# A graph network on one core: another order for ScalarE and VectorE in the last pass over the edges

## The chip, the core and the metric

The kernel runs on one core of a Trainium2 chip. Five engines work side by side and meet by semaphores: TensorE (PE, matrix products and transposes), VectorE (DVE), ScalarE (ACT), GpSimd (POOL, here the issuer of gathers and scatters) and SyncE (SP, the issuer of plain transfers). Each engine runs its own instructions strictly in the order in which they were written. The metric is device time in microseconds for one execution, lower is better.

## The reference

50,000 nodes carry 256 features, 12,500 edges carry 128. Two layers follow one another, each with a residual and a layer norm. The first weighs each edge's source row by a softmax over the edges with the same `dst`. The second averages, for each node that is named in `src`, its neighbours' rows, and is the one that matters here:

```python
    agg = segment_sum(x[nbr], dst, num_segments=n)        # dst = src list, nbr = dst list
    mean = agg / jnp.maximum(cnt, 1.0)[:, None]
    return x @ W1.T + b1 + mean @ W2.T + b2
...
edge_index = jnp.stack([src, dst])
x = _layernorm(x + _L0_gnn_ref(x, edge_index, edge_attr_128, ...), axis=-1)
x = _layernorm(x + _L1_gnn_ref(x, ..., edge_index), axis=-1)
```

## The kernel before, in words

The kernel sorts the edges by either end, runs the first layer over the edges sorted by `dst`, then a dense stage over all nodes as if none had a neighbour (`dense`, 98 groups of 512 rows), and last the SRC pass (`by_src`), which computes the rows of the nodes that do have neighbours again and scatters them over the dense result. Only the SRC pass is touched here.

The SRC pass goes over the sorted edges in Q = 25 groups of 512 (four tiles of 128, GT = 4). A group q has two inputs: the *own rows* (z rows of the nodes in `src`, gathered by POOL into `xin`, `own_rows(q)`) and the *neighbour rows* (gathered into `X` beforehand). Both want a layer norm. Own rows: VectorE takes their moments (`moments`, L971, "own statistics"), ScalarE the root (`root`, L591), VectorE the reciprocal and the offset (`invert` L985 and the `nmr` product, "own offsets"), ScalarE the normalised rows in place (L770). Then TensorE turns them (`turn_pair`, L1378), ScalarE copies the turned rows from PSUM (`own_copy`, L586), and they are a term of the products (L1389). Neighbours: VectorE makes the selection matrices `csel` and `sel` (`select_src`, L1063 and L1065) and a weight per row, ScalarE weighs the rows (`weigh_neighbours`, L750), TensorE sums them by runs (L1533), VectorE adds what is carried from one tile to the next (`sums_with_carry`, L1079 and, through the helper of L801, L1082). The products give r; VectorE takes its moments ("ended products", L971 on a bank), ScalarE the root, VectorE the reciprocal (L1250), ScalarE scales r into `yout` (`y_rows`, L596), POOL scatters it (L487).

TensorE's step q runs in two halves, p = 0 and 1, of two tiles each: turn the own rows of q-1, sum the neighbours of q, multiply q-1. VectorE and ScalarE have a step q each, 27 in all, since r of group q-2 is finished in it. So in one step an engine touches groups q-2 to q+2, and the order in which it does so is written out by hand in the three functions `by_src`. A wait stands with the instruction that needs it; whatever was written behind it waits too.

POOL's order: gather the own rows of group s+3, then scatter group s-2, in step s. A gather waits until TensorE has turned the group whose buffer it takes (four buffers); a scatter waits for `y_rows`. SP brings the sorted keys (`kB`) two groups ahead.

Of the kernel before, what the change touches and what calls it, by code (L numbers as in the profile page):

```python
# [5 lines left out]
P = 128  # L6
D = 256
DE = 128
GT = 4
# [8 lines left out]
ALU = mybir.AluOpType  # L18
# [15 lines left out]
def wait(eng, sem, value):  # L34

    if isinstance(value, int) and value <= 0:
        return
    eng.wait_ge(sem, value)
# [19 lines left out]
def build(nc, x, src, dst, edge_attr, Wn, bn, We, be, attn, W1, b1, W2, b2, out):  # L58
# [4 lines left out]
    Q = T // GT  # L63
# [19 lines left out]
    with ExitStack() as ctx:  # L83
        def sb(name, shape, dt=F32):
            return ctx.enter_context(nc.sbuf_tensor(name, shape, dt))

        def sem(name):
            return ctx.enter_context(nc.semaphore(name))

        def sems(name, n):  # L90
            return [sem(f"{name}{i}") for i in range(n)]
# [99 lines left out]
        stats = sb("stats", [P, 6, GT, 3])  # L191
        std = sb("std", [P, 6, GT])
        rstd = sb("rstd", [P, 6, GT])
        nmr = sb("nmr", [P, 2, GT])
# [87 lines left out]
        s_ost = sem("own_stats")  # L282
        s_osq = sem("own_std")
# [4 lines left out]
        s_est = sem("edge_r_stats")  # L288
        s_esq = sem("edge_r_std")
        s_enm = sem("edge_r_scales")  # L290
        s_ey = sem("edge_y_ready")
        s_xs = sems("own_z_rows_gathered", 4)
# [7 lines left out]
        s_onm = sem("own_offsets")  # L300
# [24 lines left out]
        def counted(m, u, off, n):  # L325

            return m * (4 // n) + (u + off) // n

        def in_range(q, lo, hi):
            return not isinstance(q, int) or lo <= q < hi  # L330
# [4 lines left out]
        def own_rows(q, u=0):  # L335

            if isinstance(q, int):
                return (agg[0], agg[1], aggn)[q] if q < EARLY else xin[(q + G) % 4]
            return xin[(u + G) % 4]

        def rbank(h_par, p):
            return bank[4 + 2 * h_par + p]
# [236 lines left out]
        def _(act):  # L579
# [9 lines left out]
            def root(slot, ready, n, done, rows=P):  # L589
                act.wait_ge(ready, n)  # L590
                a.activation(std[0:rows, slot, :], stats[0:rows, slot, :, 2], ACT.Sqrt, bias=eps_c[0:rows],  # L591
                             scale=1.0 / D).then_inc(done, 1)

            def y_rows(h_par, hu, slot, done, bank_of, rows=P, js=range(GT)):
                for j in js:
                    a.activation(yout[hu][0:rows, j, :], bank_of(j // 2)[0:rows, (j % 2) * D:(j % 2 + 1) * D],  # L596
                                 ACT.Copy, scale=rstd[0:rows, slot, j:j + 1]).then_inc(done, 1)
# [127 lines left out]
            def root_neighbours(q, u):  # L725
                root(4 + u % 2, s_nst, q + 1, s_nsq)
# [18 lines left out]
            def weigh_neighbours(q, u):  # L745
                act.wait_ge(s_nw, q + 1)
                wait(act, s_agg[SRC], 2 * (q - 1))
                for j in range(GT):
                    rows = X[:, bass.ds(q * GT + j, 1), 0:D].rearrange("p a c -> p (a c)")
                    a.activation(X[:, u % 2 * GT + j, 0:D], rows, ACT.Copy,  # L750
                                 scale=rstd[:, 4 + u % 2, j:j + 1]).then_inc(s_stage, 1)

            weigh_neighbours(0, 0)

            def by_src(q, m, u):
                def own_copy(p):
                    if in_range(q, 1, Q + 1):
                        turned_copy(2 + p, bank[p], s_tc, 2 * (q - 1) + p + 1,
                                    [(s_er, 2 * (q - 2) + p + 1)], s_tcc, 1.0)
                if in_range(q, 0, Q):  # L760
                    root(u % 2, s_ost, q + 1, s_osq)
                own_copy(0)
                if in_range(q, 2, Q + 2):
                    root(2 + u % 2, s_est, q - 1, s_esq)
                own_copy(1)
                if in_range(q, 0, Q):
                    act.wait_ge(s_onm, q + 1)
                    for j in range(GT):
                        row = own_rows(q, u)[:, j, 0:D]
                        a.activation(row, row, ACT.Identity, bias=nmr[:, u % 2, j:j + 1],  # L770
                                     scale=rstd[:, u % 2, j:j + 1]).then_inc(s_ex1, 1)
                if in_range(q, 0, Q - 1):
                    weigh_neighbours(q + 1, u + 1)
                if in_range(q, 0, Q - 2):
                    root_neighbours(q + 2, u)
                if in_range(q, 2, Q + 2):
                    hu = (u - 2) % 4
                    act.wait_ge(s_enm, q - 1)
                    if isinstance(q, int) and q < 6:
                        act.wait_ge(s_yst[hu], 16 * len(range(hu, G, 4)))  # L780
                    wait(act, s_ysc[hu], 16 * GT * counted(m, u, -2, 4))
                    y_rows(0, hu, 2 + u % 2, s_ey, lambda p: rbank(u % 2, p))
            steps(act, Q + 2, 4, 8, 5, by_src)


        @block.vector
        def _(dve):
# [12 lines left out]
            def stt(o, i0, s, i1, o0, o1, **kw):  # L800
                return v.scalar_tensor_tensor(out=o, in0=i0, scalar=s, in1=i1, op0=o0, op1=o1, **kw)  # L801
# [172 lines left out]
            def halves(psum):  # L974
                return psum.rearrange("p (j c) -> p j c", j=2)

            def moments(slot, pair_of, rows, done):

                pair_stats(slot, rows, 0, pair_of(0))
                pair_stats(slot, rows, 1, pair_of(1)).then_inc(done, 1)  # L980

            n_m = [0] * 4

            def invert(slot, rows, h):
                v.reciprocal(rstd[0:rows, slot, :], std[0:rows, slot, :]).then_inc(s_rc[slot], 1)  # L985
                dve.wait_ge(s_rc[slot], h)
# [65 lines left out]
            def select_src(q, m, u, off):  # L1052

                par, turn = (u + off) % 2, counted(m, u, off, 2)
                slot = 4 + par
                now = bass.ds(q * GT, GT)
                dve.wait_ge(s_nsq, q + 1)
                v.reciprocal(rstd[:, slot, :], std[:, slot, :]).then_inc(s_rc[slot], 1)
                dve.wait_ge(s_rc[slot], turn + 1)
                v.tensor_tensor(rstd[:, slot, :], rstd[:, slot, :], weight[:, now], ALU.mult).then_inc(s_nw, 1)  # L1060
                dve.wait_ge(s_kb3[SRC][par], 16 * (turn + 1))
                wait(dve, s_agg[SRC], 2 * (q - 1))
                v.tensor_tensor(csel[par][:], kB[par][:], prevk[SRC][:, now].unsqueeze(2).to_broadcast([P, GT, P]),  # L1063
                                ALU.is_equal)
                v.tensor_tensor(sel[par][:], kB[par][:], keyc[SRC][:, now].unsqueeze(2).to_broadcast([P, GT, P]),  # L1065
                                ALU.is_equal).then_inc(s_sel[SRC], 1)
# [35 lines left out]
            def neighbour_stats(q, u):  # L1102
                for p in range(2):
                    ins = pair_stats(4 + u % 2, P, p, X[:, bass.ds(GT * q + 2 * p, 2), 0:D])
                ins.then_inc(s_nst, 1)
# [122 lines left out]
            steps(dve, G, 4, 4, 6, dense, (HOOK, HOOK + APART))  # L1228
            n_m = [G // 2 + (i % 2 < G % 2) for i in range(4)]

            def by_src(q, m, u):
                slot = u % 2
                if in_range(q, 0, Q):
                    own = own_rows(q, u)
                    dve.wait_ge(s_xs[u], 16 * GT * (m + 1))
                    moments(slot, lambda p: own[:, 2 * p:2 * p + 2, 0:D], P, s_ost)
                if in_range(q, 0, Q - 1):
                    select_src(q + 1, m, u, 1)
                if in_range(q, 0, Q):
                    dve.wait_ge(s_osq, q + 1)  # L1240
                    invert(slot, P, n_m[slot] + counted(m, u, 0, 2) + 1)
                    stt(nmr[:, slot, :], stats[:, slot, :, 1], -1.0, rstd[:, slot, :], ALU.mult, ALU.mult).then_inc(s_onm, 1)
                if in_range(q, 2, Q + 2):
                    dve.wait_ge(s_er, 2 * (q - 2) + 2)
                    moments(2 + slot, lambda p: halves(rbank(slot, p)[:, :]), P, s_est)
                if in_range(q, 0, Q - 2):
                    neighbour_stats(q + 2, u)
                if in_range(q, 2, Q + 2):
                    dve.wait_ge(s_esq, q - 1)
                    v.reciprocal(rstd[:, 2 + slot, :], std[:, 2 + slot, :]).then_inc(s_enm, 1)  # L1250
                if in_range(q, 0, Q):
                    sums_with_carry(q, u)
            steps(dve, Q + 2, 4, 4, 5, by_src)


# [309 lines left out]
```

## Time and profile before

| | |
|---|---|
| Time, median of 3 runs | 1405.91 us (1404.85 to 1406.67) |
| The profiled execution | 1415.9 us, span 1414.1 us |
| PE, DVE, ACT, POOL busy | 85%, 71%, 53%, 53% of the span |
| The SRC pass in the span | from about 1056 us to the end |

The span is one profiled execution, about 10 us longer than the median. The shares are means over stages with different limits; the SRC pass is read by itself. Busy times of TensorE count a pipelined instruction as busy until its modelled end, so starts are a better measure than ends. The chain that ended last names, in order of time, the piece of work that everything after it waited for.

### The profile page before, as it was taken

Reading aid. Unit: us, or ns where it says so; the run is one execution under the profiler, and the core shown is the slowest. Engines: PE = TensorE matmul, PEld = TensorE weight load, DVE = VectorE, ACT = ScalarE, POOL = GpSimd, SP = SyncE. Lnnn points to the kernel's source line nnn. Section 1 sums busy time; section 2 is a strip of 40 time slices with the busy share of each in tenths; the row PEclk is TensorE's granted clock in tenths of the full one; section 3 lists DMA queues with packets and bytes.
Section 4 is the critical chain, followed back from the end, with each engine's and each line's share of the span. In section 5 each row is a group of like instructions: output and inputs, shape, how many; then the busy total and the mean of one; then the engine's idle time right before and its main releaser. Section 6 shows DMA issues by size and latency. Waiting matters only on the chain.

```text
span 1414.1 us, 25043 instructions
## 1 busy us (share of the span) xinstructions
PE 1201.5 (85%) x6829; PEld 1046.3 (74%) x6829; DVE 1002.8 (71%) x3483; ACT 745.4 (53%) x1743; POOL 751.7 (53%) x731
## 2 busy tenths in 40 slices
PE   5988968991099999949999999999988888888884
PEld 5977857880078888838888888888877777777773
DVE  8377897989455555349999999999985556555551
ACT  3754664550034444427777766667674544545442
POOL 1047772777767777744444106555541555555533
PEclk9989999996589999979999999999998889988887
DMA  6868887979436666657777768999961323222211
GB/s 213 272 150 206 208 225 184 272 231 348 171 68 93 101 94 92 72 137 246 239 240 245 248 241 296 310 321 325 325 238 51 91 94 94 86 91 88 93 47 43
DMA packets 118160, 254.11 MB, mean 180 GB/s; under 512 B 23705, under 2 KB 63272, under 8 KB 118084
## 3 DMA queue, kind: packets, MB, share of 16 engines
q1 hardware_dynamic: 75738, 187.26, 41.8%
q0 software_dynamic: 40128, 64.45, 20.1%
q10 hardware_dynamic: 2218, 1.53, 0.3%
q8 instruction: 30, 0.49, 0.2%
q14 instruction: 46, 0.38, 0.1%
HBM read 175.67 MB, written 130.44 MB: 216 GB/s over the span
## 4 chain that ended last, share of the span: by engine, by line
PE 70%; DVE 11%; DMA 6%; ACT 5%; issue 5%; POOL 1%; SPq 0%; DVEq 0%; ACTq 0%; POOLq 0%
PE bank L1389 41%; PE bank L1378 8%; PE bank L1366 5%; DVE stats L971 4%; PE bank L1438 3%; PE bank L1288 3%; PE bank L1442 3%; DMA X<-in_x,idx_src 3%; DVE X L798 2%; ACT aggn L633 2%; PE bank L1533 2%; ACT sel L687 1%; PE bank L1325 1%; DVE xT L801 1%; DVE xin L798 1%
## 5 line engine op out<-in xcount | busy, mean ns | idle before, releaser
L1389 PE MATMUL bank<-w1T,xT 128*128 128x256 f32 x1968 | 480.3, 392 | 2.0 <-ACT yout L596 2.0
L1389 PEld LDWEIGHTS bank<-w1T,xT 128*128 128x128 f32 x1968 | 378.0, 197 | 56.6 <-ACT xT L586 3.0
L494 POOL DMA_INDIRECT order_scratch<-pay,rank_i x200 | 194.6, 973 | 220.6 <-DVE xin L798 90.3
L586 ACT ACTIVATE xT<-bank 128x512 f32<-128x512 f32 x296 | 176.7, 598 | 91.5 <-PE bank L1378 87.0
L596 ACT ACTIVATE yout<-bank,rstd 128x256 f32<-128x256 f32 x492 | 203.8, 480 | 0.7 <-DVE rstd L1037 0.5
L591 ACT ACTIVATE std<-stats,eps_c 128x4 f32<-128x4 f32 x271 | 80.5, 298 | 230.5 <-DVE stats L971 230.4
L534 POOL DMA_INDIRECT z_scratch<-xin,idx_out x100 | 156.3, 1563 | 53.8 <-ACT xin L713 30.6
L971 DVE BATCH_NORM_STATS2 stats<-bank 128x6 f32<-128x512 f32 x246 | 167.9, 691 | 10.2 <-PE bank L1389 10.1
L971 DVE BATCH_NORM_STATS2 stats<-xin 128x6 f32<-128x512 f32 x240 | 154.6, 686 | 22.6 <-DMA xin<-z_scratch 22.6
L1389 PE MATMUL bank<-w2T,xT 128*128 128x256 f32 x400 | 126.7, 446 | 50.4 <-ACT xT L586 41.8
L487 POOL DMA_INDIRECT out_rows<-yout,idx_out x100 | 102.4, 1024 | 107.7 <-ACT yout L596 83.0
L1366 PE MATMUL bank<-sel,agg 128*128 128x196 f32 x800 | 157.0, 341 | 0.1
L801 DVE SCALAR_TENSOR_TENSOR xT<-csel,xT,bank 128x128 f32<-128x128 f32 x198 | 55.6, 342 | 139.4 <-PE bank L1389 126.3
L1378 PE MATMUL bank<-ident,xin 128*128 128x128 f32 x960 | 128.9, 274 | 19.6 <-DVE xin L798 19.6
L1378 PEld LDWEIGHTS bank<-ident,xin 128*128 128x128 f32 x960 | 114.3, 142 | 34.4 <-issue 19.9
L1389 PEld LDWEIGHTS bank<-w2T,xT 128*128 128x128 f32 x400 | 84.9, 222 | 69.2 <-issue 31.8
L798 DVE TENSOR_SCALAR xin<-xin,stats,rstd 128x256 f32<-128x256 f32 x392 | 136.0, 409 | 0.1
L1366 PEld LDWEIGHTS bank<-sel,agg 128*128 128x128 f32 x800 | 134.4, 196 | 0.6 <-DVE bank L801 0.3
L484 POOL DMA_INDIRECT X<-z_scratch,idx_dst x100 | 96.1, 961 | 69.1 <-DVE xin L798 29.7
L484 POOL DMA_INDIRECT X<-in_x,idx_src x100 | 99.0, 990 | 51.2 <-issue 20.7
L484 POOL DMA_INDIRECT xin<-z_scratch,idx_src x88 | 84.7, 963 | 76.2 <-PE bank L1378 53.8
L1288 PE MATMUL bank<-X 128*128 128x196 bf16 x800 | 96.2, 255 | 28.8 <-ACT sel L687 18.6
(249 smaller groups left out, 1765.7 us busy)
## 6 DMA issues: line engine op xcount, KB each, us to landing
z_scratch<-in_x SPq DMA_DIRECT2D x125, 400.0 KB
xin<-z_scratch SPq DMA_DIRECT2D x97, 512.0 KB, 4.8
out_rows<-yout SPq DMA_DIRECT2D x97, 512.0 KB, 3.7
kB<-sorted_scratch SPq DMA_DIRECT2D x50, 256.0 KB, 3.4
yout<-low_digits_scratch SPq DMA_DIRECT2D x50, 128.0 KB
yout<-keys_scratch SPq DMA_DIRECT2D x50, 128.0 KB, 5.7
yout<-in_edge_attr SPq DMA_DIRECT2D x12, 512.0 KB, 6.2
order_scratch<-pay,rank_i POOLq DMA_INDIRECT x200
```

The lines of the kernel that those rows point to most:

```text
L484: g.indirect_dma_start(out=dst_ap, out_offset=None, in_=table, in_offset=where).then_inc(s, 16)
L487: g.indirect_dma_start(out=table, out_offset=where, in_=src_ap, in_offset=None, bounds_check=N - 1, oob_is_err=False).then_inc(s, 16)
L494: g.indirect_dma_start(out=order_dram[k], out_offset=bass.IndirectOffsetOnAxis(ap=rank_i[k][:, t:t + 1], axis=0), in_=pay[:, t, :], in_off ...
L534: g.indirect_dma_start(out=z_dram, out_offset=column(idx_out[DST], GT * q + j), in_=xin[q % 4][:, j, :], in_offset=None, compute_op=ALU.ad ...
L586: a.activation(xT[dst_i][:].rearrange("p a b c -> p (a b c)"), src_bank[:, :], ACT.Copy, bias=raised).then_inc(copied, 1)
L596: a.activation(yout[hu][0:rows, j, :], bank_of(j // 2)[0:rows, (j % 2) * D:(j % 2 + 1) * D], ACT.Copy, scale=rstd[0:rows, slot, j:j + 1]). ...
L798: return v.tensor_scalar(o, i, s1, s2, o0, o1) if o1 is not None else v.tensor_scalar(o, i, s1, s2, o0)
L971: return v.bn_stats(stats[0:rows, slot, 2 * p:2 * p + 2, :].rearrange("p j s -> p (j s)"), pair.rearrange("p j c -> p c j"))
L1288: ins = mm(o[:, b * HC:(b + 1) * HC], onehot_lo[:, t, b * P:(b + 1) * P], onehot_hi[:, t, :], start=False, stop=False, skip_group_check=True)
L1366: ins = mm(bank[3 + t % 4][:, 0:HC], onehotT[n % 2][:, b, j * P:(j + 1) * P], table[i % 2][:, b, :], start=b == 0, stop=b == 1)
L1378: ins = tr(o[:, at:at + n], buf[0:n, 2 * p + jj, c * P:(c + 1) * P], ident[0:n, 0:n])
L1389: ins = mm(to, buf[:, jj, c, 0:n], w[:, c, :], start=not bias and i == 0 and c == 0, stop=i == len(terms) - 1 and c == 1)
```

## The change

In the SRC pass three orders are written anew. VectorE takes the own statistics and offsets of group q+1 in step q, with those of group 0 ahead of the loop; its step begins with the moments of the ended products. ScalarE begins its step with the first copy of the turned rows, normalises the own rows, takes the two roots, splits `y_rows` in two around the second copy, and weighs the neighbours last. TensorE, POOL and SP keep their order, and no instruction is added or taken away except that `y_rows` is issued in two parts of two rows.

```diff
--- before.py
+++ after.py
@@ -750,6 +750,7 @@
                     a.activation(X[:, u % 2 * GT + j, 0:D], rows, ACT.Copy,
                                  scale=rstd[:, 4 + u % 2, j:j + 1]).then_inc(s_stage, 1)
 
+            root(0, s_ost, 1, s_osq)
             weigh_neighbours(0, 0)
 
             def by_src(q, m, u):
@@ -757,29 +758,34 @@
                     if in_range(q, 1, Q + 1):
                         turned_copy(2 + p, bank[p], s_tc, 2 * (q - 1) + p + 1,
                                     [(s_er, 2 * (q - 2) + p + 1)], s_tcc, 1.0)
-                if in_range(q, 0, Q):
-                    root(u % 2, s_ost, q + 1, s_osq)
+
+                def last_step(p):
+                    if in_range(q, 2, Q + 2):
+                        y_rows(0, (u - 2) % 4, 2 + u % 2, s_ey, lambda b: rbank(u % 2, b), P, (2 * p, 2 * p + 1))
                 own_copy(0)
-                if in_range(q, 2, Q + 2):
-                    root(2 + u % 2, s_est, q - 1, s_esq)
-                own_copy(1)
                 if in_range(q, 0, Q):
                     act.wait_ge(s_onm, q + 1)
                     for j in range(GT):
                         row = own_rows(q, u)[:, j, 0:D]
                         a.activation(row, row, ACT.Identity, bias=nmr[:, u % 2, j:j + 1],
                                      scale=rstd[:, u % 2, j:j + 1]).then_inc(s_ex1, 1)
+                if in_range(q, 2, Q + 2):
+                    root(2 + u % 2, s_est, q - 1, s_esq)
                 if in_range(q, 0, Q - 1):
-                    weigh_neighbours(q + 1, u + 1)
-                if in_range(q, 0, Q - 2):
-                    root_neighbours(q + 2, u)
+                    root((u + 1) % 2, s_ost, q + 2, s_osq)
                 if in_range(q, 2, Q + 2):
                     hu = (u - 2) % 4
                     act.wait_ge(s_enm, q - 1)
                     if isinstance(q, int) and q < 6:
                         act.wait_ge(s_yst[hu], 16 * len(range(hu, G, 4)))
                     wait(act, s_ysc[hu], 16 * GT * counted(m, u, -2, 4))
-                    y_rows(0, hu, 2 + u % 2, s_ey, lambda p: rbank(u % 2, p))
+                last_step(0)
+                own_copy(1)
+                last_step(1)
+                if in_range(q, 0, Q - 1):
+                    weigh_neighbours(q + 1, u + 1)
+                if in_range(q, 0, Q - 2):
+                    root_neighbours(q + 2, u)
             steps(act, Q + 2, 4, 8, 5, by_src)
 
 
@@ -1228,26 +1234,35 @@
             steps(dve, G, 4, 4, 6, dense, (HOOK, HOOK + APART))
             n_m = [G // 2 + (i % 2 < G % 2) for i in range(4)]
 
+            def own_stats(q, m, u):
+                own = own_rows(q, u)
+                dve.wait_ge(s_xs[u % 4], 16 * GT * (m + u // 4 + 1))
+                moments(u % 2, lambda p: own[:, 2 * p:2 * p + 2, 0:D], P, s_ost)
+
+            def own_offsets(q, m, u):
+                slot = u % 2
+                dve.wait_ge(s_osq, q + 1)
+                invert(slot, P, n_m[slot] + counted(m, u, 0, 2) + 1)
+                stt(nmr[:, slot, :], stats[:, slot, :, 1], -1.0, rstd[:, slot, :], ALU.mult, ALU.mult).then_inc(s_onm, 1)
+
+            own_stats(0, 0, 0)
+            own_offsets(0, 0, 0)
+
             def by_src(q, m, u):
                 slot = u % 2
-                if in_range(q, 0, Q):
-                    own = own_rows(q, u)
-                    dve.wait_ge(s_xs[u], 16 * GT * (m + 1))
-                    moments(slot, lambda p: own[:, 2 * p:2 * p + 2, 0:D], P, s_ost)
-                if in_range(q, 0, Q - 1):
-                    select_src(q + 1, m, u, 1)
-                if in_range(q, 0, Q):
-                    dve.wait_ge(s_osq, q + 1)
-                    invert(slot, P, n_m[slot] + counted(m, u, 0, 2) + 1)
-                    stt(nmr[:, slot, :], stats[:, slot, :, 1], -1.0, rstd[:, slot, :], ALU.mult, ALU.mult).then_inc(s_onm, 1)
                 if in_range(q, 2, Q + 2):
                     dve.wait_ge(s_er, 2 * (q - 2) + 2)
                     moments(2 + slot, lambda p: halves(rbank(slot, p)[:, :]), P, s_est)
-                if in_range(q, 0, Q - 2):
-                    neighbour_stats(q + 2, u)
+                if in_range(q, 0, Q - 1):
+                    own_stats(q + 1, m, u + 1)
                 if in_range(q, 2, Q + 2):
                     dve.wait_ge(s_esq, q - 1)
                     v.reciprocal(rstd[:, 2 + slot, :], std[:, 2 + slot, :]).then_inc(s_enm, 1)
+                if in_range(q, 0, Q - 1):
+                    select_src(q + 1, m, u, 1)
+                    own_offsets(q + 1, m, u + 1)
+                if in_range(q, 0, Q - 2):
+                    neighbour_stats(q + 2, u)
                 if in_range(q, 0, Q):
                     sums_with_carry(q, u)
             steps(dve, Q + 2, 4, 4, 5, by_src)
```

On VectorE one step near the end of the loop held this before (`xin3` own rows of group q, `bank6` and `bank7` the products of group q-2, `X` neighbours of group q+2, `xT` turned sums of group q):

```order
L971 BN_STATS stats<-xin3 128x6 x2
L1058 RECIPROCAL rstd<-std 128x4
L1060 TENSOR_TENSOR rstd<-rstd,weight 128x4
L1063 TENSOR_TENSOR csel0<-kB0,prevk1 128x512
L1065 TENSOR_TENSOR sel0<-kB0,keyc1 128x512
L985 RECIPROCAL rstd<-std 128x4
L801 SCALAR_TENSOR_TENSOR nmr<-stats,rstd 128x4
L971 BN_STATS stats<-bank6 128x6
L971 BN_STATS stats<-bank7 128x6
L971 BN_STATS stats<-X 128x6 x2
L1250 RECIPROCAL rstd<-std 128x4
```

The same step in the changed kernel (`xin0` are now the own rows of group q+1):

```order
L977 BN_STATS stats<-bank6 128x6
L977 BN_STATS stats<-bank7 128x6
L977 BN_STATS stats<-xin0 128x6 x2
L1260 RECIPROCAL rstd<-std 128x4
L1064 RECIPROCAL rstd<-std 128x4
L1066 TENSOR_TENSOR rstd<-rstd,weight 128x4
L1069 TENSOR_TENSOR csel0<-kB0,prevk1 128x512
L1071 TENSOR_TENSOR sel0<-kB0,keyc1 128x512
L991 RECIPROCAL rstd<-std 128x4
L807 SCALAR_TENSOR_TENSOR nmr<-stats,rstd 128x4
L977 BN_STATS stats<-X 128x6 x2
```

The moments of the two banks stand first and the own statistics behind them, where before the own statistics stood first; `L1250` moved from behind the neighbours' moments to ahead of the selection.

On ScalarE a step of the loop before (`xT2` and `xT3` take the two halves of the turned rows, the three roots on `std` are those of the own rows, of the ended products and of the neighbours):

```order
L591 ACTIVATE std<-stats,eps_c 128x4
L586 ACTIVATE xT2<-bank0 128x512
L591 ACTIVATE std<-stats,eps_c 128x4
L586 ACTIVATE xT3<-bank1 128x512
L770 ACTIVATE xin2<-xin2,nmr,rstd 128x256 x4
L750 ACTIVATE X<-X,rstd 128x256 x4
L591 ACTIVATE std<-stats,eps_c 128x4
L596 ACTIVATE yout2<-bank4,rstd 128x256 x2
L596 ACTIVATE yout2<-bank5,rstd 128x256 x2
```

and in the changed kernel:

```order
L586 ACTIVATE xT2<-bank0 128x512
L770 ACTIVATE xin2<-xin2,nmr,rstd 128x256 x4
L591 ACTIVATE std<-stats,eps_c 128x4 x2
L596 ACTIVATE yout2<-bank4,rstd 128x256 x2
L586 ACTIVATE xT3<-bank1 128x512
L596 ACTIVATE yout2<-bank5,rstd 128x256 x2
L750 ACTIVATE X<-X,rstd 128x256 x4
L591 ACTIVATE std<-stats,eps_c 128x4
```

The root of the own rows stood ahead of the first copy and that of the ended products ahead of the second; now no root stands ahead of the first copy, both stand between the normalising and `y_rows`, and the weighing of `X` stands behind all copies.

## Rows read from the trace of the kernel before

**Rows 1.** The chain that ended last: start us, length us, what; SRC pass.

```profile
1063.29 3.69 PE bank L1389 x16
...
1171.09 3.72 PE bank L1389 x16
...
1181.04 1.22 DVE stats L971 x2
1182.49 0.58 ACT xT L586
1183.11 5.41 PE bank L1389 x16
1188.52 0.44 PE bank L1378 x4
1188.96 0.89 PE bank L1533 x8
1189.85 3.53 PE bank L1389 x16
...
1386.34 3.69 PE bank L1389 x16
```

**Rows 2.** Busy time by window: TensorE's granted clock after DVE, ACT and POOL.

```profile
700.00:1050.00 350.00, 347.93 (x1924) 307.49 (x1924) 325.39 (x820) 246.46 (x640) 150.84 (x158) 1.00 0.82 279
...
1185.00:1186.00 1.00, 1.00 (x4) 0.82 (x3) 1.00 (x3) 0.30 (x1) 0.69 (x2) 0.50 0.83 205
```

**Rows 3.** Timeline of one step, ScalarE and VectorE: start us, length us, instruction.

```profile
1189.00 0.60 ACT L586 ACTIVATE xT<-bank 128x512 f32<-128x512 f32 x1 [3.19 <-PE bank L1378]
...
1189.49 2.06 ACT L770 ACTIVATE xin<-xin,nmr,rstd 128x256 f32<-128x256 f32 x4
...
1191.46 1.69 ACT L750 ACTIVATE X<-X,rstd 128x256 f32 x4
...
1193.24 1.53 ACT L596 ACTIVATE yout<-bank,rstd 128x256 f32<-128x256 f32 x4
...
1193.56 1.12 DVE L801 SCALAR_TENSOR_TENSOR xT<-csel,xT,bank 128x128 f32<-128x128 f32 x4 [3.71 <-PE bank L1389]
...
1194.60 1.29 DVE L971 BATCH_NORM_STATS2 stats<-xin 128x6 f32<-128x512 f32 x2
...
1195.93 0.30 ACT L591 ACTIVATE std<-stats,eps_c 128x4 f32<-128x4 f32 x1 [1.16 <-DVE stats L971]
...
1196.41 0.69 DVE L1063 TENSOR_TENSOR csel<-kB,prevk 128x512 f32<-128x512 f32 x1
...
1196.76 1.13 PE L1389 MATMUL bank<-w2T,xT 128*128 128x256 f32 x4 [2.07 <-ACT xT L586]
...
1197.01 0.69 DVE L1065 TENSOR_TENSOR sel<-kB,keyc 128x512 f32<-128x512 f32 x1
...
1197.62 0.17 DVE L985 RECIPROCAL rstd<-std 128x4 f32<-128x4 f32 x1
...
1197.90 1.29 DVE L971 BATCH_NORM_STATS2 stats<-bank 128x6 f32<-128x512 f32 x2
...
1199.11 1.27 DVE L971 BATCH_NORM_STATS2 stats<-X 128x6 f32 x2
...
1200.29 0.16 DVE L1250 RECIPROCAL rstd<-std 128x4 f32<-128x4 f32 x1
```

**Rows 4.** SRC pass by line and form on POOL: count, busy us, mean ns, idle before.

```profile
L487 POOL DMA_INDIRECT out_rows<-yout,idx_out x82 | 84.6, 1032 | 65.4 <-ACT yout L596 46.5 <-issue 18.9
L484 POOL DMA_INDIRECT xin<-z_scratch,idx_src x72 | 69.1, 960 | 57.5 <-PE bank L1378 39.6 <-issue 17.8
```

**Rows 5.** Timeline of POOL in the SRC pass.

```profile
1094.49 0.98 POOL L484 DMA_INDIRECT xin<-z_scratch,idx_src  x1 [0.30 <-issue]
...
1265.89 1.44 POOL L487 DMA_INDIRECT out_rows<-yout,idx_out  x1 [0.30 <-issue]
```

**Rows 6.** Transfers by issuing line: count, us from issue to landing.

```profile
xin<-z_scratch,idx_src POOLq DMA_INDIRECT x88, 2.8
```

## The prediction

> **What bounds the kernel now.** I read the chain that ended last first, because the shares of busy time are means over stages with different limits. In the SRC pass it repeats every four pieces [rows 1]: VectorE's statistics, a ScalarE copy, TensorE's products, and again. Follow one step from 1183.11: products of the first half 5.41 us, then with no gap a turn (0.44), the neighbour sums (0.89) and the products of the second half (3.53), which end at 1193.38. I call such an end E. Then TensorE stands: the timeline shows it idle 2.07 us until 1196.76, released by the copy of the turned rows [rows 3]. A step is 1196.76 - 1183.11 = 13.65 us.
>
> What TensorE waits for is in the order of the other two engines. VectorE ends the carried sums, which need E, at E+1.22, and only then takes the own statistics (1194.60 to 1195.81). ScalarE's next instruction is the root of exactly these (1195.93), and the copy of the turned rows, whose data lay ready at about E+0.44, stands behind that root. So the copy waits for statistics that it doesn't need.
>
> The second thing to see is that the same sixteen products take 5.41 us in the first half and 3.53 in the second. The windows show why: the granted clock was 0.50 at 1185 to 1186, the lower level of 1.2 GHz, after the idle time, and 1.00 over 350 us of the dense stage, where TensorE was busy 347.93 [rows 2]. One step started at 1171.09 without that drop (3.72 for the sixteen) and ended at 1183.11, 12.02 us later [rows 1]. So of a step 2.07 us is idle and 5.41 - 3.53 = 1.88 us is slow clock; the rest is work: 2 x (0.44 + 0.89 + 3.53) = 9.72. The parts add up to 13.67, against 13.65 seen.
>
> **The change part by part.** All walks are in us after E, with start-to-start distances of rows 1 and 3.
>
> *The first copy goes to the head of ScalarE's step.* The turn ends at 0.44; in the second half of before the copy follows 0.04 behind the turn (1188.52 + 0.44 to 1189.00) and takes 0.60, so it ends at 1.08, while the neighbour sums keep TensorE busy until 1.33. That half ran without a gap in before [rows 1], and the first half now has the same neighbours. Idle time 2.07 to 0, and with it the slow clock, 1.88 to 0, as the dense stage shows for work without gaps. What is late next?
>
> *VectorE.* Carried sums of the second half 0.18 to 1.22; ended products 1.22 to 2.43 (1.21, from 1197.90 to 1199.11); own statistics to 3.64; reciprocal for y about 3.8; neighbours' reciprocal and weight to 4.4 (0.60, from 1195.81 to 1196.41); csel and sel to 5.6; own offsets to 5.9 (0.28); neighbours' moments to 7.1 (1.18); carried sums of the first half to 8.1. TensorE asks for these at 9.72 + 0.44 = 10.16. So 7.9 us of work stand in 9.72, and the slack is 2 us.
>
> *ScalarE.* First copy 0.48 to 0.97, normalising to 2.94 (1.97, to 1191.46), root of the ended products to about 3.2, root of the own rows when the statistics are written, 3.7 to 4.0, half of the y rows to 4.8 (half of 1.53). The second turn ends at 4.86 + 0.44 = 5.30, so the second copy runs 5.34 to 5.94, before the sums end at 6.19. Then y to 6.6, the weighing to 8.3 (1.69), the neighbours' root to 8.6. The next first copy is due at 10.2. The smallest slack anywhere is here: y must be out of the way by 5.30 and is at 4.8. The weighing, moved last, is wanted at 10.2 and costs nothing; if its cover were gone it would cost up to 1.69 a step.
>
> *The own rows are asked for a step earlier.* The gather of group s+3 is released by the second turn of step s, at 5.30. Four gathers start 1.26 apart (0.96 + 0.30 of gap), so the last starts 3.8 later and lands 2.8 after that [rows 4 to 6]: 11.9. The statistics want it two steps on, at 2 x 9.72 + 2.43 = 21.9. That is 9.9 us of slack where before had a step more.
>
> *POOL.* No operation is added, but it has less time. A step costs four gathers and four scatters, 4 x (0.960 + 0.30) + 4 x (1.032 + 0.30) = 10.37 us [rows 4]; that the gap is 0.30 also between a scatter and a gather when nothing is waited for, the row at 1094.49 shows [rows 5]. 10.37 is more than 9.72: POOL, idle for a quarter of each step before, becomes the longest engine by 0.65 us. The lag starts at about step 4 (the first scatter is in step 2, and the gathers ahead of it are long done) and grows until the last gather, in step 21: 17 x 0.65 = 11 us, of which 9.9 is slack. I take 1 us. Bounds: 0 (if the two means come down by 5%) and, with one issue of each step as long as the slowest row, 1.44 against 1.032 [rows 5], 17 x 1.06 - 9.9 = 8 us. After step 21 only scatters are left, 5.3 us a step, so the end of the pass is as before.
>
> The Trainium skill ("SBUF — State Buffer", section "Who interferes with whom") says that a VectorE instruction with two SBUF inputs shuts out a GpSimd instruction that reads SBUF, wholly, until it ends. The row of 1.44 us, next to csel and sel, fits a part of that; by the full rule a step of POOL would be longer by both selections, which is the second rival below.
>
> *Ahead of the loop.* VectorE now has the own statistics and offsets of group 1 between those of group 0 and the first sums: 1.21 + 0.28, and a root of 0.30 between. Between 0 (hidden where TensorE's first products wait anyway) and 1.8; I take 0.9.
>
> *The sum.* The first half's products start at 1063.29 in step 1 and at 1386.34 in step 25 [rows 1]: 323.1 us for 24 steps. By the walk they take 24 x 9.72 = 233.3. Saved 89.8, less 1 for POOL and 0.9 for the start: 87.9. What follows the last products doesn't change. The profiled execution took 1415.9 us; less 87.9 it is 1328.0. The median of the runs is 0.9929 of it (1405.91), so I forecast 1319 us.
>
> **Rivals.**
> 1. The second copy comes late: y's first half waits for its reciprocal, which waits behind the own statistics, and these for a gather. For it: the slack is only 0.5 us. Against: every term on that path is a row. If it ran over by 1 us, TensorE would stand 0.5 us a step: 24 x 0.5 = 12, 1331. If that also dropped the clock, 24 x (0.5 + 1.88) = 57, 1376.
> 2. POOL becomes the bound early, since csel and sel (0.60 each, start to start) hold up its issues in full. Then a step of POOL is 10.37 + 1.21 = 11.58, the lag 1.86 a step, 17 x 1.86 - 9.9 = 22 us instead of 1: 1340. For it: the 1.44 row. Against: the mean scatter, 1.032, already stands beside these two in before, and is far from 1.6. It is to this that the skill's rule leads; the rows bear out a third of it at most (1.44 - 1.032 = 0.41 of 1.21).
> 3. Nothing is gained: TensorE finds another wait of 2 us in the first half, say the carried sums, and drops its clock as before: 1406. For it, only that VectorE's order is rewritten; against it the slack of 2 us.
> 4. Slower. The own rows are now asked for before the y rows' reciprocal, so a late gather stops VectorE, y, the second copy and TensorE together, and POOL's pace becomes everybody's. It decides from the point where a step of POOL exceeds 13.65: eight issues of 1.41 on the mean beside the gaps of 0.30. If all eight were as slow as the slowest row, 1.44, a step would be 13.9 and the pass 24 x 0.27 = 6 us longer: 1412. The means of 0.96 and 1.03 speak against it.
>
> **How the numbers follow.** Forecast 0.70, with its own range 1314 to 1328 (the steps at 9.72 with no cost at all at the low end, 89.8 saved, and 2 us for what a run differs; POOL's bound of 8 at the high end). Rival 1: 0.11, rival 2: 0.14, rival 3: 0.02, rival 4: 0.03. The range for 8 in 10 takes in the short form of rival 1 and rival 2 with their margins, and leaves out the rest: 1312 to 1345. Within 0.2% is what a measurement can tell from no change, so faster 0.95, same 0.02, slower 0.03.
>
> **What would show it.** Right: TensorE's first-half products take about 3.6 instead of 5.4 us in every step, the granted clock stays near 1.00 from 1063 on, steps are 9.7 to 9.9 us, and VectorE's own wait is for TensorE ahead of the second half's sums. POOL has next to no idle time from step 5 to 21, and in the last of these VectorE begins to wait for the gather. Wrong: a step over 10.4 with POOL idle (then a wait between VectorE and ScalarE that I priced as covered is exposed), a copy of the second half that starts after y later than 0.1 us behind its turn, or issues on POOL of 1.2 us and more on the mean.

## The result and the profile after

The changed kernel takes 1323.37 us (median of 4 runs), the kernel before 1405.38 in the same session. The ratio is 0.9413, 95% interval 0.9392 to 0.9433: faster. The forecast was 1319, the range 1312 to 1345. In some executions of either kernel (one of these four) a stage long before the SRC pass takes some 45 us longer; the ratios and the table below leave such executions out, and where a profile has it, only its SRC pass is read.

The rows below are of a second execution of the changed kernel, 1321.7 us long (span 1319.9). Its lines are numbered a little differently: the turn is L1393 (was L1378), the products L1404 (L1389), the neighbour sums L1548 (L1533), the moments L977 (L971), the carried sums L807 (L801). First the chain that ended last, in the same columns as [rows 1]:

```profile
1055.09 4.24 PE bank L1404 x16
...
1142.55 0.44 PE bank L1393 x4
1142.99 0.89 PE bank L1548 x8
1143.88 3.52 PE bank L1404 x16
1147.40 0.44 PE bank L1393 x4
1147.84 0.89 PE bank L1548 x8
1148.73 3.52 PE bank L1404 x16
...
1235.56 0.45 PE bank L1393 x4
...
1237.49 0.50 POOL xin L484
...
1270.54 0.95 POOL xin L484
...
1271.80 2.82 DMA xin<-z_scratch,idx_src
...
1274.64 1.32 DVE stats L977 x2
...
1277.01 0.49 ACT xT L586
...
1277.55 3.72 PE bank L1404 x16
...
1292.16 3.69 PE bank L1404 x16
```

From step 1 until 1236.01 every piece is TensorE's and starts where the one before it ends; VectorE and ScalarE, which took turns with TensorE in [rows 1], are gone. Then the chain passes over ScalarE's y rows to POOL and stays there from 1237.49 to 1271.49, one issue behind the other with gaps of 0.30 us, until a gather that lands late holds up VectorE (1274.64). So near the end of the pass it is POOL that everything waits for. From step 1 (1055.09) to step 25 (1292.16) the first-half products are 237.07 us apart; in [rows 1] the same two were 323.05 apart. That is 85.98 us, somewhat more than the 82.0 between the two medians; from step 25 to the end of the span both kernels take 27.7 us.

The busy time by window, with TensorE first and the granted clock behind POOL as in [rows 2]:

```profile
1090.00:1140.00 50.00, 50.00 (x285) 44.74 (x285) 39.39 (x109) 35.25 (x89) 38.42 (x39) 1.00 0.39 124
1140.00:1190.00 50.00, 50.00 (x286) 44.83 (x285) 39.23 (x109) 35.33 (x89) 38.42 (x39) 1.00 0.39 116
...
1240.00:1290.00 50.00, 48.61 (x279) 43.41 (x278) 32.84 (x93) 31.86 (x78) 38.67 (x38) 1.00 0.32 104
```

In the first two windows TensorE is busy all the time, and its clock is 1.00 in all three. POOL is at its end too: 38.42 us in 39 issues, and 39 gaps of 0.30 make 50.1.

One step on the timeline, to set beside [rows 3] (E, the end of the second half's products, is at 1103.32 by the chain):

```profile
1103.79 0.60 ACT L586 ACTIVATE xT<-bank 128x512 f32<-128x512 f32 x1 [1.82 <-PE bank L1393]
...
1103.88 1.12 DVE L807 SCALAR_TENSOR_TENSOR xT<-csel,xT,bank 128x128 f32<-128x128 f32 x4 [2.30 <-PE bank L1404]
1104.92 1.28 DVE L977 BATCH_NORM_STATS2 stats<-bank 128x6 f32<-128x512 f32 x2
1106.12 1.28 DVE L977 BATCH_NORM_STATS2 stats<-xin 128x6 f32<-128x512 f32 x2
...
1107.44 0.30 ACT L591 ACTIVATE std<-stats,eps_c 128x4 f32<-128x4 f32 x1 [0.90 <-DVE stats L977]
1107.64 0.82 ACT L596 ACTIVATE yout<-bank,rstd 128x256 f32<-128x256 f32 x2
1108.64 0.60 ACT L586 ACTIVATE xT<-bank 128x512 f32<-128x512 f32 x1 [0.17 <-PE bank L1393]
1109.13 0.83 ACT L596 ACTIVATE yout<-bank,rstd 128x256 f32<-128x256 f32 x2
1109.84 1.70 ACT L750 ACTIVATE X<-X,rstd 128x256 f32<-128x256 f32 x4
```

The first copy follows E by 0.47 us, and both copies wait only for TensorE's turn. The second had 0.17 us to spare here, after y's first half. This step is the tightest one: the other 18 second copies between 1069 and 1246 us waited 0.41 to 0.72 us for the turn. Behind them only the three whose y rows come late (1255.64, 1266.22 and 1276.90), after VectorE's three waits for gathered rows, follow y without a wait.

The waits from 1056 to 1300 us (who waited for whom: us, times, longest) and POOL's issues from 1092 to 1297 us by line, as in [rows 4]:

```profile
DVE xT L807 <- PE bank L1404: 50.0, 25, 3.7
...
DVE stats L977 <- DMA xin<-z_scratch,idx_src: 3.8, 3, 1.6
...
PE bank L1404 <- ACT xT L586: 1.4, 2, 0.8
```

```profile
L487 POOL DMA_INDIRECT out_rows<-yout,idx_out x84 | 86.4, 1029 | 25.6 <-issue 25.0 <-ACT yout L596 0.6
L484 POOL DMA_INDIRECT xin<-z_scratch,idx_src x70 | 68.5, 978 | 21.3 <-issue 20.4 <-PE bank L1393 0.6 <-ACT yout L596 0.3
```

VectorE waits for TensorE in every step. It waits for gathered rows only three times, near the end, and of these 3.8 us only 1.4 reach TensorE. Next to all of POOL's idle time is the gap between issues, where [rows 4] had 46.5 and 39.6 us of real waits.

### The profile page after: what moved, and what is told of

Its sections match the earlier page's. It is cut to its first block, busy times and chain, and to the rows that moved or that the text cites. A ratio compares the mean times of both kernels' runs of the same rounds, so it can differ in the third digit from the quotient of the medians.

```text
span 1368.8 us, 25051 instructions
## 1 busy us (share of the span) xinstructions
PE 1204.9 (88%) x6829; PEld 1060.4 (77%) x6829; DVE 1001.9 (73%) x3483; ACT 745.6 (54%) x1743; POOL 755.3 (55%) x731
## 4 chain that ended last, share of the span: by engine, by line
PE 71%; DVE 9%; DMA 5%; issue 5%; ACT 5%; POOL 3%; SPq 1%; ACTq 0%; POOLq 0%; DVEq 0%
PE bank L1404 38%; PE bank L1393 8%; PE bank L1381 5%; PE bank L1303 4%; PE bank L1453 3%; PE bank L1457 3%; PE bank L1548 3%; DVE stats L977 3%; PE bank L1340 3%; DMA X<-in_x,idx_src 3%; DVE X L804 2%; ACT aggn L633 2%; PE bank L1333 2%; ACT sel L687 1%; DVE xin L804 1%
## 5 line engine op out<-in xcount | busy, mean ns | idle before, releaser
L1404 PE MATMUL bank<-w1T,xT 128*128 128x256 f32 x1968 | 461.9, 381 | 1.7 <-ACT yout L596 1.6
L1404 PEld LDWEIGHTS bank<-w1T,xT 128*128 128x128 f32 x1968 | 366.0, 191 | 50.5 <-ACT xT L586 2.3
L596 ACT ACTIVATE yout<-bank,rstd 128x256 f32<-128x256 f32 x492 | 206.7, 481 | 1.2 <-DVE rstd L1260 0.7
L977 DVE BATCH_NORM_STATS2 stats<-bank 128x6 f32<-128x512 f32 x246 | 167.9, 691 | 10.9 <-PE bank L1404 10.8
L977 DVE BATCH_NORM_STATS2 stats<-xin 128x6 f32<-128x512 f32 x240 | 154.5, 686 | 25.9 <-DMA xin<-z_scratch 22.1
L1393 PE MATMUL bank<-ident,xin 128*128 128x128 f32 x960 | 128.9, 274 | 19.6 <-DVE xin L804 19.5
L1393 PEld LDWEIGHTS bank<-ident,xin 128*128 128x128 f32 x960 | 114.4, 142 | 34.6 <-issue 20.1
L1303 PE MATMUL bank<-X 128*128 128x196 bf16 x800 | 110.9, 281 | 29.0 <-ACT sel L687 17.0
L484 POOL DMA_INDIRECT X<-in_x,idx_src x100 | 99.1, 991 | 50.1 <-issue 19.6
L1303 PEld LDWEIGHTS bank<-X 128*128 128x128 bf16 x800 | 79.2, 112 | 56.6 <-ACT sel L687 32.1
L1404 PE MATMUL bank<-w2T,xT 128*128 128x256 f32 x400 | 107.5, 392 | 2.8 <-ACT xT L586 1.4
L807 DVE SCALAR_TENSOR_TENSOR bank<-iota_f,dig_f,bank 128x196 f32<-128x196 f32 x200 | 84.6, 423 | 32.9 <-PE bank L1381 32.7
```

The costliest lines, as they stand in the source:

```text
L484: g.indirect_dma_start(out=dst_ap, out_offset=None, in_=table, in_offset=where).then_inc(s, 16)
L977: return v.bn_stats(stats[0:rows, slot, 2 * p:2 * p + 2, :].rearrange("p j s -> p (j s)"), pair.rearrange("p j c -> p c j"))
L1303: ins = mm(o[:, b * HC:(b + 1) * HC], onehot_lo[:, t, b * P:(b + 1) * P], onehot_hi[:, t, :], start=False, stop=False, skip_group_check=True)
L1393: ins = tr(o[:, at:at + n], buf[0:n, 2 * p + jj, c * P:(c + 1) * P], ident[0:n, 0:n])
L1404: ins = mm(to, buf[:, jj, c, 0:n], w[:, c, :], start=not bias and i == 0 and c == 0, stop=i == len(terms) - 1 and c == 1)
```

## The experiments

Each theory was that of the prediction: the stall of 2.07 us comes from the place of ScalarE's first copy, and the slow clock from the stall. The rivals were that another wait stands behind it, that the clock has another cause, that the other parts carry the gain, and that POOL sets the pace. Since the early stages differ by several us from one execution to the next, this table gives the SRC pass by itself beside the times: from the first-half products of step 1 to those of step 24 by the timeline, 23 steps.

| Kernel | 23 steps, us | a step | median time, us | ratio to before, interval |
|---|---|---|---|---|
| before | 311.64 | 13.55 | 1405.38 | |
| changed, second execution | 227.56 | 9.89 | 1323.01 | 0.9421 [0.9381, 0.9460] |
| changed, third | 226.65 | 9.85 | 1324.67 | 0.9403 [0.9365, 0.9442] |
| one_swap | 242.09 | 10.53 | 1336.79 | 0.9506 [0.9476, 0.9537] |
| filled_gap | 311.27 | 13.53 | 1416.77 | 1.0071 [1.0043, 1.0100] |
| filled_gap4 | 275.11 | 11.96 | 1374.57 | 0.9758 [0.9712, 0.9804] |
| ended_first | 342.46 | 14.89 | 1438.5 (two runs) | |
| weigh_before_y | 251.61 | 10.94 | 1346.96 | 0.9573 [0.9521, 0.9625] |
| extra_gather | 249.61 | 10.85 | 1345.14 | 0.9543 [0.9485, 0.9601] |
| scatter_later | 227.10 | 9.87 | 1324.45 | 0.9396 [0.9356, 0.9436] |

**The changed kernel once more, twice** (after_again and after_third, no edit). Expected:

> The changed kernel unchanged, timed once more beside the others. Expected: 1321 to 1326 us, TensorE steps of 9.7 to 9.9 us in the SRC pass and about 10.6 us in the last three with a gather, in which VectorE waits 0.8 to 1.6 us for the gathered rows.

> The changed kernel once more, as the neighbour of the next runs on the same chip: 1320 to 1325 us.

Both agree with the first result. (Of the last three steps with a gather, two took 10.5 and 10.7 us, the third 9.8.) Their stretches of 23 steps differ by 0.9 us, which is what such a stretch can tell.

**one_swap: the first copy alone is moved.** The kernel before with one line in another place:

```diff
                     turned_copy(2 + p, ...)
+                own_copy(0)
                 if in_range(q, 0, Q):
                     root(u % 2, s_ost, q + 1, s_osq)
-                own_copy(0)
```

> The kernel before with a single change: on ScalarE the root of the own rows stands behind the first copy of the turned rows instead of ahead of it. Theory (the stall is the place of that root alone, the rest is what keeps a new stall from coming up): the 2.07 us go, but the y rows at the end of ScalarE's step now run until 11.9 us after E and hold the next first copy, and the second copy waits for the root of the ended products (6.0 against 5.3); steps of about 10.8 us if the clock stays up through gaps of 1 us and 0.5 us, 12.7 if it drops as before: 1337 to 1382 us. Rival (all of the gain needs VectorE's new order, since the statistics are what is late): no change, 1400 to 1406.

311.64 - 242.09 = 69.6 of the change's 84.1 us. The timeline shows what is left (L1389 and the others by the numbers of before), and one window the clock:

```profile
1248.15 1.53 ACT L596 ACTIVATE yout<-bank,rstd 128x256 f32<-128x256 f32 x4
1249.58 0.59 ACT L586 ACTIVATE xT<-bank 128x512 f32<-128x512 f32 x1
...
1250.22 1.13 PE L1389 MATMUL bank<-w2T,xT 128*128 128x256 f32 x4 [0.61 <-ACT xT L586]
```

```profile
1200.00:1250.00 50.00, 47.12 (x270) 41.64 (x268) 35.67 (x99) 33.76 (x84) 38.42 (x39) 1.00 0.35 114
```

The copy starts when the four rows of `y_rows` end, so TensorE stands 0.61 us; such waits come 20 times and make 12.4 us. The clock stays at 1.00. The time is at the low end of the range expected, since the second wait that it priced (0.5 us, behind the root of the ended products) did not come. The other parts of the change together take the rest away (84.1 - 69.6 = 14.5 us); how much of it is VectorE's new order and how much ScalarE's, no run separates.

**filled_gap and filled_gap4: the stall is filled, not removed.** The kernel before, with products that nothing reads put between the first half's neighbour sums and the waits for the carried sums and the copy, which move behind them; 9 in one, 4 in the other:

```diff
-                        pe.wait_ge(s_carry, 8 * h + 4 * p + 4)
-                        pe.wait_ge(s_tcc, 2 * h + p + 1)
                         wait(pe, s_ey, GT * (h - 2) + 2 * p + 2)
...
+                        if p == 0:
+                            for _ in range(9):
+                                mm(rbank((u - 1) % 2, 0)[:, 0:D], ident[:], w1T[:, 0, :], start=True, stop=True)
+                        pe.wait_ge(s_carry, 8 * h + 4 * p + 4)
+                        pe.wait_ge(s_tcc, 2 * h + p + 1)
```

> The kernel before with nine more matrix products of 0.216 us in TensorE's gap of 2.07 us, written into the bank that the next product clears anyway; they add no result. Theory (1.88 us of each step are a clock that drops because TensorE stood idle): the clock stays at 1.00, the sixteen products of the first half take 3.6 us, a step 11.8 instead of 13.65: about 1361 us, though no wait was taken away. Rival (the first half is slow because VectorE and ScalarE use the same memories at that time): 1404 to 1410.

> The kernel before with four more fp32 products (eight instructions of 0.216 us, 1.73 us in all) in TensorE's gap, in place of the nine (eighteen instructions, 4.05 us) of the earlier run, which overfilled it. Theory (1.88 us of a step are the clock that falls after the idle time): the clock stays at 1.00, a step is about 11.8 us, 24 x 1.88 = 45 us less: about 1361 us. Rival (the slow products have another cause): 1404 to 1410.

TensorE's timeline with 9, the sixteen products behind the filling:

```profile
1204.65 4.05 PE L1542 MATMUL bank<-w1T,ident 128*128 128x256 f32 x18
1208.54 1.03 PE L1389 MATMUL bank<-w2T,xT 128*128 128x256 f32 x4
1209.40 1.03 PE L1389 MATMUL bank<-w1T,xT 128*128 128x256 f32 x4
...
1211.99 0.60 PE L1378 MATMUL bank<-ident,xin 128*128 128x128 f32 x4
```

and with 4, with one of its windows:

```profile
1203.20 1.13 PE L1389 MATMUL bank<-w2T,xT 128*128 128x256 f32 x4 [0.28 <-ACT xT L586]
...
1212.93 1.89 PE L1542 MATMUL bank<-w1T,ident 128*128 128x256 f32 x8
1215.17 1.13 PE L1389 MATMUL bank<-w2T,xT 128*128 128x256 f32 x4 [0.34 <-ACT xT L586]
```

```profile
1200.00:1250.00 50.00, 48.61 (x272) 42.51 (x271) 33.07 (x90) 28.73 (x72) 32.24 (x33) 1.00 0.33 105
```

The first was badly sized: a product appears as two instructions, and 4.05 us is twice the stall. Its sixteen products took 3.45 us (1208.54 to 1211.99) in place of 5.41, with the clock at 1.00, and the longer filling cost as much: no gain in the SRC pass, and 1416.77 us in all (1.0071) where 1361 had been expected. Where those 10 us over the kernel before arise, the profile, of the fastest of its runs, does not show. The second is the clean one. It takes no wait away, adds work, and is 36.5 us faster over 23 steps; a step of 11.97 is 9.72 + 1.89 + 0.34, to 0.02. VectorE and ScalarE do the same work beside the first-half products as before, and these take 3.56 us (second half's 1220.06, less turn and sums of 1.33, less 1215.17) in place of 5.41, which speaks against the rival. So the slow clock followed from TensorE standing still, and is a loss of its own beside the stall. The expected 1361 was 13.6 us too low. Two terms of that are in the traces, about 4.6 us each: a step takes 11.96 and not 11.77, since filling and remaining wait (2.23) are longer than the stall (2.07); and not every step of before lost 1.88 us (its 24 steps take 13.46 on the mean, the step that was read 13.65). The other 4 us are not assigned.

**ended_first: VectorE's new beginning alone.** The kernel before with the moments of the ended products ahead of the own statistics, which are still those of the same step:

```diff
             def by_src(q, m, u):
                 slot = u % 2
+                if in_range(q, 2, Q + 2):
+                    dve.wait_ge(s_er, 2 * (q - 2) + 2)
+                    moments(2 + slot, ...)
                 if in_range(q, 0, Q):
...
-                if in_range(q, 2, Q + 2):
-                    dve.wait_ge(s_er, 2 * (q - 2) + 2)
-                    moments(2 + slot, ...)
```

> The kernel before with VectorE's half of the change in its smallest form: the moments of the ended products ahead of the own statistics of the same group, nothing else. Theory (what counts is what stands ahead of the first copy): the own statistics come 1.21 us later, the root and the copy behind them too, a step 14.9 us: about 1434 us. Rival (VectorE's order is what helps): faster than 1400.

```profile
1221.59 0.30 ACT L591 ACTIVATE std<-stats,eps_c 128x4 f32<-128x4 f32 x1 [2.46 <-DVE stats L971]
1221.79 0.59 ACT L586 ACTIVATE xT<-bank 128x512 f32<-128x512 f32 x1
...
1222.52 2.07 PE L1389 MATMUL bank<-w2T,xT 128*128 128x256 f32 x4 [3.48 <-ACT xT L586]
1224.39 1.91 PE L1389 MATMUL bank<-w1T,xT 128*128 128x256 f32 x4
```

As expected, the stall grew by 1.2 us, the length of the moments put ahead (1.21 start to start): from 2.07 to 3.26 in most steps, and from 2.25 to 3.48 in every fourth, of which the step shown is one. The slow clock stayed in most steps. The time, 1438.5 us, was expected at 1434. This is the same chain (own statistics, root, copy) made longer, and it shows that this part is no gain by itself. VectorE's other new order, the own statistics a step earlier, was not tried alone.

**weigh_before_y: the weighing put back.** The changed kernel with `weigh_neighbours` ahead of the y rows:

```diff
                     root((u + 1) % 2, s_ost, q + 2, s_osq)
+                if in_range(q, 0, Q - 1):
+                    weigh_neighbours(q + 1, u + 1)
 ...
                 last_step(1)
-                if in_range(q, 0, Q - 1):
-                    weigh_neighbours(q + 1, u + 1)
```

> The changed kernel with the weighing of the neighbours (1.70 us on ScalarE) put back ahead of the rows y, behind the two roots, everything else as changed. Theory (ScalarE's second copy has only some 0.5 us of slack, so the place of the weighing is a necessary part of the change): the second copy ends about 1.26 us after the moment at which TensorE has ended its first sixteen products, TensorE idles about that long in front of the first-half or the second-half products in each of some 24 steps, with the granted clock at 1.00, since idle stretches of 0.5 to 0.7 us did not lower it in the earlier run: about 30 us more than the changed kernel, 1353 us. If such an idle stretch lowers the clock as the one of 2.07 us before the change did, 1.88 us more a step: up to 1398. Rival (the weighing's place is indifferent, the order of copy and roots alone does it): the time of the changed kernel, 1321 to 1327.

```profile
1156.35 1.71 ACT L750 ACTIVATE X<-X,rstd 128x256 f32 x4 [0.32 <-DVE rstd L1066]
1157.96 0.81 ACT L596 ACTIVATE yout<-bank,rstd 128x256 f32<-128x256 f32 x2
1158.67 0.58 ACT L586 ACTIVATE xT<-bank 128x512 f32<-128x512 f32 x1
...
1159.31 1.13 PE L1404 MATMUL bank<-w2T,xT 128*128 128x256 f32 x4 [1.28 <-ACT xT L586]
```

```profile
1150.00:1200.00 50.00, 45.27 (x256) 40.07 (x255) 34.02 (x92) 30.22 (x74) 35.32 (x37) 1.00 0.32 105
```

The wait is 1.28 us in the step shown (1.26 were worked out). It stands in front of the second-half products in 20 steps, with 0.79 to 1.35 us, 21.6 in all (two earlier steps wait 0.82 each for carried sums); 30 were expected, and the 23 steps are 24 us longer than in the changed kernel. The clock did not fall. Rival 1, the late second copy, is thus a real mechanism, here without a slow clock, as in its short form; the change stays clear of it by the place of the weighing.

**extra_gather: POOL made longer.** The changed kernel with one more gather of 128 rows in each step, whose rows nothing reads:

```diff
...
                     gather_own(q)
+                    wait(pool, s_extra, 16 * (q - EARLY))
+                    gather(v_b[:], z_dram, column(idx_src[SRC], GT * q), s_extra)
...
```

> The changed kernel with one more gather a step on POOL (1.26 us), into a tile that nothing reads. Theory (POOL is 0.65 us a step over TensorE, and the gathers have 9.9 us of slack): the lag grows by 1.91 us a step, 17 x 1.91 - 9.9 = 22.6 us late in place of 1: about 1343 us. Rival (POOL is hidden behind TensorE): 1321 to 1325.

```profile
DVE stats L981 <- DMA xin<-z_scratch,idx_src: 24.8, 11, 2.7
```

```profile
1314.19 1.13 PE L1408 MATMUL bank<-w2T,xT 128*128 128x256 f32 x4 [1.79 <-ACT xT L590]
...
1326.05 1.12 PE L1408 MATMUL bank<-w2T,xT 128*128 128x256 f32 x4 [1.89 <-ACT xT L590]
1327.01 1.72 PE L1408 MATMUL bank<-w1T,xT 128*128 128x256 f32 x4
1328.53 1.91 PE L1408 MATMUL bank<-w2T,xT 128*128 128x256 f32 x4
```

22 us more over 23 steps, and the waits for gathered rows in the SRC pass go from 3.8 to 24.8 (here read from 1110 to 1345 us). So POOL sets the pace as soon as its step grows by 12%: the changed kernel has no room left there. The late rows reach TensorE over VectorE, y and the second copy, the path of rival 4. Eight such waits of 1.61 to 1.79 us, from 1232 to 1314, left the clock at 1.00; behind the one of 1.89 it was 0.50 (1328 to 1330), and behind one of 1.98 (1349.73) again.

**scatter_later: POOL's tail is moved.** The changed kernel with each group's scatter one group later in POOL's order, so that the gathers go out earlier:

```diff
...
-            for q in range(EARLY, Q + 5):
+            for q in range(EARLY, Q + 6):
...
-                if q >= 5:
-                    h = q - 5
+                if q >= 6:
+                    h = q - 6
...
```

> The changed kernel, with each scatter of finished rows one group later in POOL's order. Theory (late in the pass the gathers come late because POOL's eight issues a step take longer than TensorE's step; the scatters have time, the gathers don't): POOL has 5.3 us less ahead of the last gathers, VectorE's waits for gathered rows (0.8 to 1.6 us in three steps) go, and with them two idle stretches of TensorE of 0.6 to 0.7 us: about 1.6 us less than the changed kernel. Rival (those gathers are late for another reason, such as the landing): no change, or a longer tail.

```profile
DVE stats L977 <- DMA xin<-z_scratch,idx_src: 2.5, 2, 1.5
```

The waits were to go; of 3.7 us in the changed kernel's third execution 2.5 remain, and the time shows no difference to it (1324.45 against 1324.67). Why two of the three waits stay is open. An effect of 1 us is below what the runs tell. No version here beats the changed kernel.

## Why the prediction was right

**The stall and the slow clock.** Right, and shown. The copy behind the root of the own statistics was what TensorE waited for: one line moved gives 69.6 us, one more thing ahead of it costs 30.8. That the slow clock follows from the stall was argued from [rows 2]; filled_gap4 shows it. From step 2 on the first-half products take 3.5 to 3.7 us instead of 5.41. A stall of 2.07 us did not lower the clock each time: the step at 1171.09, which the prediction names, began after one and kept 3.72.

**VectorE.** Right. It was given 2 us of slack; it waits 50.0 us for TensorE in 25 waits, 2.0 on the mean (2.30 in the step shown).

**ScalarE.** Right: the second copy was to have 0.5 us of slack, and it has 0.41 to 0.72 in 18 of the 19 steps named above. In the step shown it has 0.17: there VectorE's carried sums begin 0.56 after E instead of 0.18, the root of the own rows, which stands ahead of y, waits for them (0.90), and y's first half starts 4.3 us after E; in the 13 other steps read from 1113 to 1231 us it starts at 3.9 to 4.1, where 4.0 was predicted. Rival 1 stood this half microsecond away, and the weighing's place decided over it.

**The gathers and POOL.** Right. The mean issues are 1.029 and 0.978 us where 1.032 and 0.960 stood in the sum; a POOL step is 4 x (1.029 + 0.30) + 4 x (0.978 + 0.30) = 10.43 us (10.37 predicted). The lag used up the slack only at the end, where the chain runs through POOL, and cost TensorE 1.4 us (1 predicted, bounds 0 and 8). Rival 2, issues shut out in full beside the two selections (11.58 a step), did not come. The sentence of the Trainium skill ("SBUF — State Buffer", section "Who interferes with whom") that led to it is borne out in part only: beside one of the two selections 15 gathers took 1.05 us on the mean and 21 scatters 1.12, beside none 55 gathers 0.96 and 63 scatters 1.00 (the longest issue 1.42). That is 4 us over some 20 steps, 0.2 a step where the full rule had 1.21.

**The sum.** 237.07 us for the 24 steps against 233.3 and the 1 us for POOL: 2.8 more. Step 1, whose first products still run at a slower clock (4.24 us against 3.52; granted 0.50 from 1054.8 to 1056), makes 0.7 of it, and the 0.9 set aside for the start covers that; POOL makes 0.4 (1.4 against 1). The other 1.7, a term left out, are product groups that take 3.58 to 3.70 instead of 3.52, half of them from step 4 on. What lengthens these product groups no run here shows. So 85.98 us were saved where 87.9 were forecast, and this makes 1.9 of the 4.4 us by which the median (1323.4) lies above the forecast (1319). For the rest, 1405.9 less 86 would be 1320, and the measured medians lie 3 to 5 us above that. In the stages ahead of the SRC pass, which the change doesn't touch, the two profiles shown differ by 8.2 us (step 1 at 1063.29 and at 1055.09), so these few us can't be assigned. Taking the profile to the median by a factor of 0.9929 spread the profile's surplus over all stages, though these 8.2 us lie ahead of the SRC pass; it changed little (1318.6, where 1405.9 - 87.9 is 1318.0).

## What to carry to other kernels

An engine here runs its instructions in the order in which they were written, so ask of every wait on it what stands behind; here a copy whose data was ready 0.44 us after E waited for statistics that it didn't need, and moving that one line gave four fifths of the gain. The parts of a reordering don't add: VectorE's new beginning alone cost 31 us, and the place of the weighing, which by the prediction's sum saved nothing, guarded 24. Fill a stall once with idle work of its own length: the difference tells how much of the loss is the clock and how much the wait.

## What the runs showed of the hardware

- TensorE's granted clock stayed at 1.00 with waits of 0.3 us a step (filled_gap4), 0.5 to 0.7 (one_swap), 0.8 to 1.35 (weigh_before_y) and 1.61 to 1.79 (extra_gather, eight steps running); behind waits of 1.89 and 1.98 in extra_gather it fell to 0.50. With waits of 1.96 to 2.26 a step (before: 0.91, 0.88, 0.86 and 0.88 over the four windows from 1150 to 1350) the products behind the wait ran slow in 22 of 23 steps, with 3.16 to 3.48 (ended_first: 0.87, 0.86, 0.90, 0.83) in 18 of 23. Only from 1.89 us on did a wait here cost twice, and not each time.
- An f32 product with 256 columns stands in the trace as two matmul instructions of some 0.22 us each: nine make x18 and 4.05 us, four x8 and 1.89.
- POOL's step was 10.43 us in a pass whose steps took 9.88; gathers asked for early enough hid all but 1.4 us of the difference over 24 steps, and one gather more in each step no longer fit.
